# Loading the replicated queries through ScalarE's DMA queue

## The reference

```python
x = x + xattn(layernorm(x), ctx)          # 16 heads of 64, 64 context rows a batch
xn = layernorm(x)
# dense path: causal attention with 16 heads of 16, then a gated net
q, k, v = xn @ wq, xn @ wk, xn @ wv
scores = where(causal, q @ k.T / sqrt(16), min)
o = softmax(scores) @ v
h = xn + rmsnorm(o @ wo)
dense = h + rmsnorm((silu(h @ w1) * (h @ w3)) @ w2)
# sparse path: 8 experts, the 2 best of each token
topw, topi = top_k(softmax(xn @ router_w), 2)
moe = rmsnorm(sum(topw * expert_out[topi]))
out = x + dense + moe
```

## Time and profile before

| | us |
|---|---|
| median of 3 runs | 1718.03 |
| lowest and highest | 1711.98, 1718.67 |
| the profiled execution | 1725.52 |
| its span in the trace | 1723.7 |
| PE busy | 1407.8 (82% of the span) |
| DVE, ACT, POOL busy | 845.5, 543.7, 503.4 |
| one middle batch (first L436 issue to that of the next) | 164.1 |

### The profile page before, as it was taken

The page is one execution under the profiler, slowest core; times in us unless marked ns, Lnnn a source line. Parts: engine busy times, 40 slices in busy tenths (PEclk is TensorE's granted clock), DMA queues, the critical chain, the costliest instruction groups (busy, mean ns, idle before and its releaser), DMA issues.

```text
span 1723.7 us, 25491 instructions
## 1 busy us (share of the span) xinstructions
PE 1407.8 (82%) x7721; PEld 955.2 (55%) x7722; DVE 845.5 (49%) x1877; ACT 543.7 (32%) x1018; POOL 503.4 (29%) x680
## 2 busy tenths in 40 slices
PE   7765896899788978897889789878978789999930
PEld 3542565567555755675467556655655465666620
DVE  0445463646464546545555556454636423333347
ACT  3230532152225214430532053215321413333322
POOL 3123043204411340323032303330432013555532
PEclk9885999899889989998999889989997889999975
DMA  5314105010501050014102310401040352222247
GB/s 215 127 49 87 26 1 125 10 38 0 131 4 37 2 129 19 21 35 99 38 1 61 74 38 0 105 30 38 1 122 13 114 87 68 85 85 85 86 165 256
DMA packets 107072, 116.68 MB, mean 68 GB/s; under 512 B 39416, under 2 KB 80912, under 8 KB 107024
## 3 DMA queue, kind: packets, MB, share of 16 engines
q1 hardware_dynamic: 88080, 98.10, 20.3%
q0 software_dynamic: 8576, 17.87, 3.3%
q10 hardware_dynamic: 10368, 0.04, 0.3%
HBM read 71.36 MB, written 44.21 MB: 67 GB/s over the span
## 4 chain that ended last, share of the span: by engine, by line
PE 56%; issue 19%; DMA 7%; POOL 5%; DVE 5%; SPq 4%; ACT 3%; ACTq 0%; POOLq 0%; DVEq 0%
PE ps L892 9%; PE ps L925 7%; PE ps L763 6%; DMA room<-parts_d 5%; PE ps L746 5%; PE ps L900 5%; PE ps L775 3%; PE ps L942 3%; PE ps L813 3%; SPq L436 3%; PE ps L715 2%; PE ps L877 2%; PE ps L734 2%; PE ps L668 2%; PE ps L687 2%
## 5 line engine op out<-in xcount | busy, mean ns | idle before, releaser
L813 PE MATMUL ps<-room 96*128 96x128 bf16 (+3 forms) x512 | 151.2, 353 | 118.3 <-DMA room<-parts_d 88.1
L892 PE MATMUL ps<-hT,w 128*128 128x512 f32 x768 | 205.6, 418 | 9.7 <-DVE gT L1406 8.3
L1055 ACT ACTIVATE room<-ps 128x1024 f32<-128x1024 f32 x160 | 159.5, 1023 | 143.5 <-PE ps L847 140.0
L1355 DVE TENSOR_REDUCE nm<-ps 128x2 f32<-128x256 f32 (+3 forms) x160 | 127.0, 823 | 104.7 <-PE ps L814 101.8
L892 PEld LDWEIGHTS ps<-hT,w 128*128 128x128 f32 x768 | 148.1, 196 | 47.0 <-DVE gT L1406 9.0
L813 PEld LDWEIGHTS ps<-room 96*128 96x128 bf16 x512 | 55.0, 108 | 180.7 <-issue 119.3
L1077 ACT ACTIVATE th<-ps 128x512 f32<-128x512 f32 x64 | 38.3, 598 | 364.5 <-PE ps L892 364.5
L925 PE MATMUL ps<-room 128*128 x288 | 137.2, 599 | 3.5 <-ACT room L1092 3.5
L845 PE MATMUL ps<-room 99*128 99x512 bf16 (+3 forms) x512 | 127.0, 323 | 8.9 <-DMA room<-mT 6.3
L900 PE MATMUL ps<-w,gT 128*128 128x256 f32 x512 | 121.4, 380 | 0.4 <-DVE gT L1406 0.4
L562 POOL TENSOR_TENSOR ve_a<-mv,eps 128x1 f32<-128x1 f32 (+1 forms) x40 | 9.9, 247 | 376.5 <-DVE mv L1240 247.7
(11 more groups left out here) (216 smaller groups left out, 2554.7 us busy)
## 6 DMA issues: line engine op xcount, KB each, us to landing
room<-parts_d SPq DMA_DIRECT2D x96, 256.0 KB, 7.0
room<-xs_d SPq DMA_DIRECT2D x72, 128.0 KB, 2.0
room<-pair_d SPq DMA_DIRECT2D x8, 1024.0 KB, 7.5
room<-in_L_ffn_ew SPq DMA_DIRECT2D x24, 256.0 KB, 6.2
xin<-in_x SPq DMA_DIRECT2D x8, 512.0 KB, 4.0
parts_d<-xnT SPq DMA_DIRECT2D x32, 128.0 KB, 1.8
parts_d<-o_tok SPq DMA_DIRECT2D x32, 128.0 KB, 1.8
parts_d<-oT SPq DMA_DIRECT2D x32, 128.0 KB, 1.7
```

The lines of the kernel that those rows point to most:

```text
L813: mm(bank(o, n), q_rep[0:KREP, rep_at(h), t * P:n], k_rep[0:KREP, rep_at(h), 0:n], start=True, stop=False)
L892: last = mm(bank(up_banks(b, m)[i]), w[:, x, k, m * P:(m + 1) * P], hT[:, y, k, :], start=((x, y, k) == terms[0]), stop=((x, y, k) == term ...
L1055: done(fn(prob[:, grp % 2, u * 1024:(u + 1) * 1024], ps[:, n % 2 * 1024:n % 2 * 1024 + 1024], ACT.Exp), "b_exp")
L1355: done(v.tensor_reduce(nm[:, t, 2 * hp:2 * hp + 2], pair_ps, AX.X, ALU.max, negate=True), "a_max")
```

## The change

The six loads of q leave SP's stream. ACT issues them in its step `route`, right behind the exponential, after it has waited for the same events (`q_out`, and that the scores of the batch before no longer read `q_rep`). SP then waits for `k_out` alone and issues the six loads of k. Bytes, shapes, sources and destinations of all twelve stay as they are.

```diff
-                    for which, part_of, rep, out_name, name in ((0, Q_PART, q_rep, "q_out", "rep_q"), (1, K_PART, k_rep, "k_out", "rep_k")):
-                        if c is None:
-                            sp.wait_ge(p0["split"], 2)
-                        need(sp, b, out_name, per[out_name])
-                        for j in range(NREP):
-                            src = parts_d[part_of[j], which, :, :, :].rearrange("(h d) a n -> d h (a n)", d=HD)
-                            done(sp.dma_start(rep[j:KREP:NREP, :, :].rearrange("d (h a) n -> d h (a n)", a=KD), src), name, 16)
+                    if c is None:
+                        sp.wait_ge(p0["split"], 2)
+                    need(sp, b, "k_out", per["k_out"])
+                    for j in range(NREP):
+                        src = parts_d[K_PART[j], 1, :, :, :].rearrange("(h d) a n -> d h (a n)", d=HD)
+                        done(sp.dma_start(k_rep[j:KREP:NREP, :, :].rearrange("d (h a) n -> d h (a n)", a=KD), src), "rep_k", 16)
...
                         done(fn(g_b, g_a, ACT.Exp), "gexp")
+                        if c is None:
+                            act.wait_ge(p0["split"], 2)
+                        else:
+                            need(act, c, "b_ps", per["b_ps"])
+                        need(act, b, "q_out", per["q_out"])
+                        for j in range(NREP):
+                            src = parts_d[Q_PART[j], 0, :, :, :].rearrange("(h d) a n -> d h (a n)", d=HD)
+                            done(act.dma_start(q_rep[j:KREP:NREP, :, :].rearrange("d (h a) n -> d h (a n)", a=KD), src), "rep_q", 16)
```

## The result

The changed kernel takes 1689.68 us (median of four runs, 1683.8 to 1693.45) against 1716.94 us for the kernel before (four runs, 1711.98 to 1718.67): 27 us less, a ratio of 0.984 with a 95% interval of 0.980 to 0.988. The forecast was 1714 us and the range ended at 1695, so the prediction was wrong by its size. The profiled execution of the changed kernel has a span of 1682.0 us, against 1723.7.

What follows compares the result with a forecast made beforehand. The prediction took the transfers of the replicating loads, which PE waits for, as the bound. Issues 0, stream 0, ACT 0 and tail -4 us took the 1718 us median to 1714 us, range 1695 to 1735.

Steps and rivals of the forecast that it cites:

- The bound: PE's wait before the first score product: the last load's landing sets the batch's end, microsecond for microsecond; transfers bound, not issuing.
- ACT's issues and what stands behind them: On ACT after the exponential: six issues at 0.65 us delay tanh, `slots` and scatters, all under PE's wait: 0 us.
- The cover: PE's wait for the loads, hiding its later block: at least 7.7 us remain of 8.92 or more.
- The stream of transfers: The twelve replicating loads: still 1.20 us each from the same start, so they end where they ended: 0 us gained.
- rival of faster draining: Two queues move the twelve loads faster: 4.8 us less in eight batches, 38 us, 1680 us; chance 0.06.
- The tail: Late last landing beside POOL's scatters, some 23 us in all: keeps its size but for 0.5 us in seven batches, 4 us.
- The tail goes: At the last landing: the last load may be confirmed before the scatters write, 12 to 23 us less; chance 0.27.
- got in sooner: POOL's scatters, served earlier between the loads of two queues: 8 to 26 us slower, 1726 to 1744; chance 0.15.
- ACT's issues were not dear: Rival on ACT's load issues: at 3 us each, PE is late by 6.6 us in seven batches, 1764 us; chance 0.05.

Runs made afterwards that it cites:

- e4: The changed kernel, but ACT issues all twelve loads, those of k behind the wait for their stores, and SP none: 1687 us, ratio 0.981.
- e1: The kernel before, with POOL beginning its scatters only when all twelve replicating loads have landed: 1696 us, ratio 0.986.
- f1: The kernel before, with thirteen idle one-element multiplications on POOL ahead of its first scatter, which comes 1.9 us later: 1701 us, ratio 0.991.
- e2: The changed kernel, with POOL beginning its scatters only when all twelve loads have landed: 1687 us, ratio 0.981.
- e3: The kernel before, with SP issuing a load of q and one of k in turn, behind the stores of both: 1744 us, ratio 1.015.
- f2: The changed kernel, with ACT's six loads behind the tanh of block 3, so that the scatters keep their old time: 1721 us, ratio 1.004.
- f3: The changed kernel, with two of ACT's six loads moved ahead, between its copies of v: 1700 us, ratio 0.990.
- f4: The changed kernel with two of ACT's loads moved ahead between its copies of v, and scatters held until all twelve loads land: 1689 us, ratio 0.984.

## Why the prediction was wrong

**The bound.** Right, for this change. PE waits at this place for the last landing, and 4.2 us in seven batches are 29, where 27 were measured. That every microsecond there is one of the time is too strong: e4 lands 0.8 us a batch later than the changed kernel, lets PE come later still, and is as fast. That issuing is not the bound was right too: e1 and f1 leave SP's twelve issues as they were and gain 22 and 14 us.

**ACT's issues and what stands behind them.** Right in kind: 0.65 us predicted for an issue, 0.7 measured (4.20 us for six); the tanh 2.4 us later in relation to the exponential (2.0 predicted), all of it covered. The cover was mis-sized, since the loads land 3.6 us sooner and the lower clock makes PE's block 4 some 1.6 us longer; 3.1 us are left, not 7.7.

**The stream of transfers.** "Twelve loads at 1.20 us therefore end where they ended" failed. Where no tail hides it, the step from the first landing to the twelfth is 1.11 to 1.14 us with loads in both queues (changed, e2) and 1.19 to 1.20 with one (e1, e4, f1), on average of batches 2 to 8. It was the rival of faster draining, priced at 4.8 us a batch and given 0.06; it is true with some 0.8 us a batch, 6 us in all by the landings and 9 by the times of e1 and e2, and not in the first batch. The argument against it, that the engines show no gap to fill, was not sound: they counted as busy all the time in either kernel, at 1.05 before and at 0.94 to 1.07 now, and the same packets went through faster. The Trainium skill's section "Issuing engines are not separate DMA queues" of "DMA: Bandwidth & Descriptors", by which only issue time is saved, does not hold on average of these batches; why, no run here shows.

**The tail.** The term that was mis-sized most. The mechanism was named rightly, by the rows (scatters beside the end of the stream), and then the sum took "a tail that keeps its size but for a part of the shift", 4 us in all. It went but for the first batch: e1, where it goes altogether, gains 22 us. The mistake was to treat the tail as something that keeps its size when the scatters' start shifts, when it depends on how long before the end of the stream they start. By the packet records, ranges of batches 2 to 8:

| | first scatter's issue to the loads' last packet, us | last packet to last landing, us |
|---|---|---|
| e3 | 10.0 to 11.1 | 3.3 to 5.7 |
| f2 | 7.6 to 10.7 | 0.9 to 4.4 |
| before | 7.9 to 8.9 | 2.1 to 5.9 |
| f3 | 6.0 to 6.8 | 0.4 to 2.7 |
| f1 | 5.8 to 6.4 | 0.5 to 0.8 |
| changed | 4.6 to 5.6 | 0.5 to 1.0 |
| e4 | 1.6 to 2.7 | 0.6 to 0.9 |
| e1, e2, f4 | no scatter yet | 0.4 to 0.9 |

With the first batches counted in, no batch below 6.4 us has a late confirmation; between 6.4 and 6.8 us three of five have one; from 7.6 on all have one of 1.9 to 5.9 us but the third of f2 (8.2 us, 0.9). The changed kernel's own first batch, whose scatters come early (8.8 us), has 2.3. The kernel before stood beyond this edge with 8.2 us on average; the 1.6 us by which the scatters shifted and the 1.3 us by which the data were through sooner made that 5.3. By these numbers neither alone would have been safely enough (6.6 and 6.9), so that the whole tail went is owed to where this kernel stood and to both effects together, of which the sum had the first alone, priced at 0.5 us a batch. That tails of 1.5 to 5.4 us in batches that are otherwise alike speak against a cost of fixed size could have been read ahead; how large the tail is beyond the edge, no row explains. The rule on order in the section "Queues, rings and completion order" of the Trainium skill's page "DMA: Bandwidth & Descriptors", that a semaphore's increment lands only after every earlier write of that engine, across its queues, fits what e1 and the packets show: loads whose data are in, confirmed late while another queue writes to DRAM. That it is this rule, engine by engine, no run here shows, and the runs moved the scatters only as a whole.

**The rivals.** "The tail goes" was the right one, given 0.27 and 12 to 23 us. With the faster draining added to it the sum would have been 1717 - 22 - 9 = 1686 us, and e2 measured 1687. The forecast was held near no change by taking the tail as nearly fixed and the faster draining at nothing. The two had been held apart as if only one could come true. The scatters hardly got in sooner (the first packet of POOL's queue started 14.1 us after the first load, before 14.8, on average of batches 2 to 8), and ACT's issues were not dear.

## What to carry to other kernels

A load that is waited for is not at an end when its data are in: here, with scatters of another queue under way beside its last microseconds, its semaphore came up to 5.9 us late. So look at the last landing for itself and hold it against the last packet, in every batch and not only in one, and try to move the stores (here by 1.9 us) first. The same holds the other way: a load issued early on a second queue can lie ahead of a store that someone waits for (f3). And where two mechanisms point the same way, add their prices in one case before the range is drawn.

## What the runs showed of the hardware that was not expected

- Loads confirmed late: in the kernel before the last semaphore came 2.1 to 5.9 us after the last packet of the loads, while POOL's scatters wrote to DRAM; with the scatters held back (e1, e2, f4) 0.4 to 0.9 us.
- Twelve loads of 256 KB in rows of 2 KB, to 16 partitions each, landed 1.19 to 1.20 us apart from one queue (e1, e4, f1) and 1.11 to 1.14 us apart from two (changed, e2), on average of batches 2 to 8; in the first batch there was no such difference.
- Stores held up beside loads: 4.7 us from a 128 KB store's issue to the release that it gave, with two loads of another queue issued shortly ahead of it and more behind it (f3), against 1.9 us before, where the first load was issued behind it.
- After only 2.73 us without work PE's clock was granted at 0.50 from 605 to 607, in the block that followed (4.62 us instead of 3.05). Before, after 1.18 us without work, the same block took its 3.05 us.
